# Cross-attention phase of a four-layer decoder kernel: order of SyncE's loads and stores, place of the residual on GpSimd, and order of two VectorE steps

## Chip, cores and metric

One Trainium2 chip, one core. The metric is the device time of one execution in microseconds (us). The kernel before was timed in three runs: median 3507.88 us, from 3506.46 to 3513.25 us. Step numbers (h), rounds (r) and line numbers below are those of the kernel before.

## The reference

Four decoder layers are applied one after the other to `x` (32 sequences of 128 tokens, 256 features), each with a context of the same shape. Layer 0 is the one in which the change lies. It has 8 heads of 128 features, and this form (cut down):

```python
Q, K, V = linear(x), linear(x), linear(x)                 # inner projections
x  = layer_norm(x0 + mha(Q, K, V, causal and pad mask))   # self attention
Q2 = linear(x); K2 = linear(context); V2 = linear(context)
y  = layer_norm(x0 + mha(Q2, K2, V2, pad mask))           # cross attention
ff = linear(relu(linear(y)))                              # 256 -> 1024 -> 256
x  = layer_norm(y + ff)
```

where `mha` projects to 8 heads, computes `softmax(q k^T / sqrt(128))` with masked keys at minus infinity, mixes the values and projects back to 256 features. `x0` is the input of the layer in both residual sums. Layers 1 to 3 (16 heads of 16 features) follow and are not touched.

## The kernel before, in words

**Phases.** `four_layers` runs four phases in turn, each a block with a program for every engine, with a barrier between them: `phase8` with `cross=False` (layer 0, self attention), `phase8` with `cross=True` (layer 0, cross attention and feed-forward; tiles named `cross_...`), then the phases `middle` and `fourth`. The diff touches `phase8`, and only what it does under `cross`.

**Rounds.** The cross phase has 8 rounds (0 to 7) of 4 sequences, that is 512 tokens. Rounds 0, 1 and 7 (`LAST`) are written out, 2 to 6 are a hardware loop on each engine. In round r the engines do three things at once, interleaved by hand in `one_round`: attention of round r, the first layer norm and the feed-forward of round r-1, and the second layer norm of rounds r-1 and r-2. Matmuls are split for precision: every operand is a high and a low part, and `product` (L90 to L99) makes three matmuls for one, all recorded as L97.

**One step h of TensorE (PE)** (h = 0 to 7, one per head, L1288 to L1329): scores of head h (L365, after a mask matmul L359); V and then K projection for head i = h+2 (`pe_v`, `pe_head`, reading the context tiles `ct_hi`, `ct_lo`); a feed-forward slot; the Q projection for head i (reading `xt_hi`, `xt_lo`); turn of the probabilities of head h (`pe_turn`, L374, four transposes); a slot; output projection of head h-1 (`pe_out`); at some h the transposes of a layer norm (L562); a slot; mix with V (`pe_mix`, L385). At h = 6 and 7 the index i wraps, and the projections are those of the next round: at h = 6 PE waits for `ct_loaded` ahead of V and for `x_loaded` ahead of Q. Feed-forward slots exist from h = 2 on, three to a step (`slot_of`): slot s makes output piece `out_of(s)` and then hidden piece `hidden_of(s)`. There are 16 hidden pieces t.

**PSUM banks** in this phase: V in bank 4, K and Q share bank 3, but Q of steps h = 0 and 1 goes to bank 2 (`spare`). Hidden pieces take banks 4, 4, 3 in turn (`HID`), so slot 12 (h = 6) writes bank 4, out of which VectorE must have taken V before. Bank 2 also holds the feed-forward output; output piece t = 8 (slot 11, h = 5) may only begin when VectorE has read the sum of pair 0 out of it (`sum2`, L179, tile `cross_z`). A claim of a bank is a wait for its last reader.

**VectorE (DVE) in a step** (L1023 to L1060): `dve_max` (L450, the row maxima of the scores), eviction of V (`dve_v`, L437), eviction of K (`dve_k`, L444), then `dve_weigh`, which takes the reciprocal of the softmax sums (L457) and multiplies the probabilities (L460, two inputs in SBUF). It waits for the exponentials on ScalarE (L417, four with an accumulator read each). PE's turn waits for L460. At h = 6 the evictions of V and K come behind `dve_weigh`. Then follow casts of hidden pieces to their high part (`dve_hi`, L531), norm sums and statistics, and last `dve_lo` (L466).

**GpSimd (POOL) in a round** (`one_round`, L1187 to L1215): three small operations for `poison`, the normalisation of the norms (`pool_hat`, L202, L205, L210), then for each hidden piece t its low part (`pool_lo`, L536), and between them `rows1`, `rows2` (L219 and L227) and, behind t = 9, `make_residual`: two TENSOR_TENSOR operations over 128x1024 (L1157 adds the output bias to `x_rows`, L1162 adds `poison`). The first of them releases `residual_sum`, the second `residual_ready`, for which VectorE waits in `sum1` at h = 0 of the next round. Behind t = 14 comes `make_flags` for the next round (L1129), behind t = 15 `rows2(Back(r, 1), 0)`.

**SyncE (SP)** issues every DMA in program order, and a wait on it holds all that is behind it. In round r of the loop: `load_round(r+1)`, then `store_rows(r-2, pair 1)`, `store_columns(r-2)`, `store_rows(r-1, pair 0)`. `load_round` under `cross` waits and issues in this order: pad (waits for `pad_flags`), `x_rows` (L765, waits for `residual_sum` of round r), context high and low (L772, wait until V and K of round r are all projected, that is for K of h = 5), x high and low (L777, wait for Q of h = 5). The two context loads are 512 KB each, as are the two of x and the two of `store_columns`. `store_columns(r-2)` waits for `norm2.lo_ready`, whose last part VectorE makes at h = 4 of round r (L587), and `store_rows(r-2, pair 1)` for `rows2` behind t = 8.

Of the kernel before, what the change touches and what calls it, by code (L numbers as in the profile page):

```python
# [85 lines left out]
def f32(ap):  # L86
    return ap.bitcast(F32)
# [564 lines left out]
def phase8(nc, tag, cross, x, ctx_t, pad, packed, cols, v_row_dram, rows, out, ctx_out, to_flag=()):  # L652
# [3 lines left out]
    with ExitStack() as ctx:  # L656
# [94 lines left out]
        def _(sp):  # L751
            def load_round(r):
                tok = bass.ds(r * TOK, TOK)
                if not cross:
# [4 lines left out]
                sp.wait_ge(pad_flags.sem, pad_flags.at(r, 0))  # L759
                kit.gated(sp)  # L760
                sp.dma_start(pad_ints[:], pad[bass.ds(r * G, G)].rearrange("b o k -> o b k")
                             .broadcast_to([P, G, SEQ])).then_inc(pad_loaded.sem, 16)
                sp.wait_ge(residual_sum.sem, residual_sum.at(r, 0))
                kit.gated(sp)
                sp.dma_start(x_rows[:], x[-1][tok, :].rearrange("(b t) f -> t b f", b=G)) \  # L765
                  .then_inc(rows_loaded.sem, 16)
                if cross:
                    sp.wait_ge(att.v_in_psum.sem, att.v_in_psum.at(r, 0))
                    sp.wait_ge(att.k_in_psum.sem, att.k_in_psum.at(r, 0))
                    kit.gated(sp)  # L770
                    for tile, src in ((ct.hi, ctx_t[0]), (ct.lo, ctx_t[1])):
                        sp.dma_start(f32(tile[:]), src[:, tok].rearrange("(c p) t -> p c t", p=P)) \  # L772
                          .then_inc(ct_loaded.sem, 16)
                    sp.wait_ge(att.q_in_psum.sem, att.q_in_psum.at(r, 0))
                    kit.gated(sp)
                    for tile, src in ((xt.hi, x[0]), (xt.lo, x[1])):
                        sp.dma_start(f32(tile[:]), src[:, tok].rearrange("(c p) t -> p c t", p=P)) \  # L777
                          .then_inc(x_loaded.sem, 16)
# [73 lines left out]
            else:  # L852
                load_round(1)
                load_round(2)
                store_rows(0, 1, 1, 0)
                with sp.Fori(2, LAST) as r:
                    load_round(r + 1)
                    store_rows(Back(r, 2), r, 2, 1)
                    store_columns(Back(r, 2), r, 2)
                    store_rows(Back(r, 1), r, 1, 0)  # L860
# [99 lines left out]
        def _(dve):  # L960
# [48 lines left out]
            def one_round(r, post, tail, more):  # L1009
# [3 lines left out]
                for h in range(H8):  # L1013
# [9 lines left out]
                    if cross and project and h != H8 - 2:  # L1023
                        att.dve_k(dve, r, psum, i, ahead)
# [2202 lines left out]
```

## Time and profile before

| what | value |
|---|---|
| three timed runs | 3506.46, 3507.88, 3513.25 us |
| the profiled execution's own time | 3517.44 us, 9.6 us above the median |
| its span | 3515.7 us |
| time outside the span | 1.7 us |
| granted clock of PE, mean of the span | 0.956 of full speed |
| busy, share of the span | PE 88%, DVE 56%, ACT 56%, POOL 47% |
| cross phase, from its first load (620.6 us) to its last store (1477.8 us) | 857 us |

How to read it: all times in the rows are us from the start of the span unless marked ns. "PE" is the matmul side of TensorE and "PEld" its weight loads, which overlap it. A time in square brackets is the idle time of that engine just before the instruction, and behind the arrow stands what ended it. Matmuls are pipelined: a row's own duration is longer than the step to the next matmul's start, so an idle time counted from the end of one to the start of the next is somewhat less than what the chain of starts loses. The granted clock is the share of full speed (2.4 GHz) at which PE ran; 0.5 is its lower level, 1.2 GHz.

### The profile page before, as it was taken

Reading aid. Unit: us, or ns where it says so; the run is one execution under the profiler, and the core shown is the slowest. Engines: PE = TensorE matmul, PEld = TensorE weight load, DVE = VectorE, ACT = ScalarE, POOL = GpSimd, SP = SyncE. Lnnn points to the kernel's source line nnn. Section 1 sums busy time; section 2 is a strip of 40 time slices with the busy share of each in tenths; the row PEclk is TensorE's granted clock in tenths of the full one; section 3 lists DMA queues with packets and bytes.
Section 4 is the critical chain, followed back from the end, with each engine's and each line's share of the span. In section 5 each row is a group of like instructions: output and inputs, shape, how many; then the busy total and the mean of one; then the engine's idle time right before and its main releaser. Section 6 shows DMA issues by size and latency. Waiting matters only on the chain. (4 is left out here: it accounts for less than half of the span.)

```text
span 3515.7 us, 81973 instructions
## 1 busy us (share of the span) xinstructions
PE 3087.0 (88%) x28275; PEld 2679.8 (76%) x28400; DVE 1985.9 (56%) x4082; ACT 1961.5 (56%) x7922; POOL 1648.8 (47%) x2002
## 2 busy tenths in 40 slices
PE   7999997799999999537999999999999999848886
PEld 5999997488888889536888888788888888745564
DVE  2455554344444444335777777777777777635665
ACT  2444443233344444226777777777777777626775
POOL 1233333114444444512566666666666666652445
PEclk8999998899999999868999999999999999979998
DMA  2222221401111110032221222233111111122321
GB/s 100 64 69 66 78 72 37 147 28 37 52 51 45 51 50 19 36 110 73 82 70 59 67 68 70 86 90 112 58 56 58 59 54 56 36 74 65 102 85 56
DMA packets 218094, 232.77 MB, mean 66 GB/s; under 512 B 41920, under 2 KB 183232, under 8 KB 215360
## 3 DMA queue, kind: packets, MB, share of 16 engines
q1 hardware_dynamic: 217920, 230.49, 20.8%
q8 instruction: 105, 1.72, 0.2%
q14 instruction: 69, 0.57, 0.1%
HBM read 148.57 MB, written 65.01 MB: 61 GB/s over the span
## 5 line engine op out<-in xcount | busy, mean ns | idle before, releaser
L1719 ACT ACTIVATE middle_stage<-middle_psum,middle_neg_max 128x128 f32<-128x128 f32 x2048 | 727.7, 386 | 358.5 <-DVE middle_neg_max L1699 358.2
L1719 ACT ACTIVATION_READ_ACCUMULATOR middle_stage<-middle_psum,middle_neg_max 128x1 f32 x2048 | 462.2, 226 | 0.0
L1699 DVE TENSOR_REDUCE middle_neg_max<-middle_psum 128x4 f32<-128x512 f32 x512 | 337.4, 681 | 63.0 <-PE middle_psum L1662 62.9
L1673 PE MATMUL middle_psum<-middle_eye,middle_stage 128*128 128x128 f32 x2048 | 322.1, 280 | 19.2 <-DVE middle_p_turned_odd L1705 9.4
L1673 PEld LDWEIGHTS middle_psum<-middle_eye,middle_stage 128*128 128x128 f32 x2048 | 232.5, 142 | 71.0 <-issue 46.5
L1621 POOL COPY middle_inverse_row<-middle_inverse 128x128 f32<-128x128 f32 x256 | 68.6, 297 | 381.6 <-DVE middle_inverse L1588 348.5
L1786 POOL TENSOR_SCALAR middle_n_z<-middle_n_z,middle_n_moments,middle_n_rstd 128x256 f32<-128x256 f32 x192 | 234.7, 1229 | 20.3 <-POOL middle_n_rstd L1781 20.3
L536 POOL TENSOR_TENSOR cross_ff_hidden_lo<-cross_ff_relu,cross_ff_hidden_hi 128x256 fp32r<-128x256 f32 x128 | 101.2, 792 | 284.9 <-DVE cross_ff_hidden_hi L531 284.9
L1901 POOL TENSOR_TENSOR middle_ff_hidden_lo<-middle_ff_relu,middle_ff_hidden_hi 128x256 fp32r<-128x256 f32 x256 | 184.2, 740 | 52.8 <-DVE middle_ff_hidden_hi L1895 52.8
L97 PE MATMUL middle_psum<-middle_n_yt_hi,middle_w_lo 128*128 128x256 f32 x640 | 194.7, 304 | 14.4 <-DVE middle_n_yt_lo L1833 9.7
L1705 DVE COPY middle_p_turned_odd<-middle_psum 128x512 f32<-128x512 f32 x256 | 174.8, 683 | 34.4 <-PE middle_psum L1673 34.3
L1705 DVE COPY middle_stage<-middle_psum 128x512 f32<-128x512 f32 x256 | 175.5, 685 | 20.8 <-PE middle_psum L1673 20.5
L1600 ACT ACTIVATE fourth_stage<-fourth_psum,fourth_neg_max 128x128 f32<-128x128 f32 x512 | 182.1, 387 | 4.1 <-DVE fourth_neg_max L1576 4.1
L97 PE MATMUL middle_psum<-middle_n_yt_hi,middle_w_hi 128*128 128x256 f32 x640 | 179.8, 281 | 0.0
L97 PE MATMUL middle_psum<-middle_n_yt_lo,middle_w_hi 128*128 128x256 f32 x640 | 179.6, 281 | 0.0
L1628 POOL TENSOR_TENSOR middle_attended_lo<-middle_mix,middle_attended_hi 128x256 fp32r<-128x256 f32 x128 | 95.0, 742 | 160.2 <-DVE middle_attended_hi L1711 160.2
L97 PE MATMUL middle_psum<-middle_w_hi,middle_ff_hidden_lo 128*128 128x256 f32 x512 | 163.7, 320 | 3.5 <-POOL middle_ff_hidden_lo L1901 3.5
L531 DVE CAST cross_ff_hidden_hi<-cross_ff_relu 128x256 fp32r<-128x256 f32 x128 | 44.6, 349 | 215.8 <-ACT cross_ff_relu L526 215.8
L526 ACT ACTIVATE cross_ff_relu<-cross_psum,cross_cols 128x256 f32<-128x256 f32 x128 | 60.8, 475 | 178.5 <-PE cross_psum L97 178.5
L1662 PE MATMUL middle_psum<-middle_stage,middle_a_q 32*128 32x256 f32 x2048 | 152.3, 413 | 0.3 <-ACT middle_stage L1719 0.2
L97 PE MATMUL middle_psum<-middle_w_lo,middle_ff_hidden_hi 128*128 128x256 f32 x512 | 145.0, 283 | 0.0
L97 PE MATMUL middle_psum<-middle_w_hi,middle_ff_hidden_hi 128*128 128x256 f32 x512 | 144.7, 283 | 0.0
(341 smaller groups left out, 10880.7 us busy)
## 6 DMA issues: line engine op xcount, KB each, us to landing
middle_stage<-middle_a_k SPq DMA_DIRECT2D x1024, 16.0 KB, 1.8
middle_xt_hi<-x_hi SPq DMA_DIRECT2D x32, 256.0 KB, 2.7
middle_xt_lo<-x_lo SPq DMA_DIRECT2D x32, 256.0 KB, 3.0
middle_ct_hi<-context_hi SPq DMA_DIRECT2D x32, 256.0 KB, 2.9
middle_ct_lo<-context_lo SPq DMA_DIRECT2D x32, 256.0 KB, 3.2
middle_x_rows<-x_rows SPq DMA_DIRECT2D x32, 256.0 KB, 2.8
middle_mask_flags<-flags SPq DMA_DIRECT2D x128, 64.0 KB, 1.9
x_rows<-middle_n_z SPq DMA_DIRECT2D x32, 256.0 KB, 2.2
```

Of the source, the lines that this page charges most:

```text
L97: ins = pe.matmul(out, w, x, start=first and n == 0, stop=last and n == total - 1, skip_group_check=skip)
L536: pool.tensor_tensor(self.hidden.lo[:, t % HIDDEN_SLOTS, :], self.relu[:, t % HIDDEN_SLOTS, :], f32(self.hidden.hi[:, t % HIDDEN_SLOTS, :] ...
L1600: ins = act.activation(self.sh.p[:, h % 4, x, :], psum[:, SCORE_BANKS[h % 4], x * SEQ:(x + 1) * SEQ], ACT.Exp, bias=self.sh.neg_max[:, h % ...
L1621: ins = pool.tensor_copy(self.sh.inverse_row[:, b, k * P:(k + 1) * P].rearrange("p (g d) -> p g d", g=8), self.sh.inverse[:, b, k * 8:(k + ...
L1628: pool.tensor_tensor(self.sh.attended.lo[:, :, b * SEQ:(b + 1) * SEQ], self.sh.mix[:, b, :].rearrange("p (c q) -> p c q", c=C), f32(self.s ...
L1662: ins = pe.matmul(banks.psum[:, bank, c * T2:(c + 1) * T2].rearrange("p (e k) -> p e k", e=2), self.proj.q[rows, c, tokens], self.proj.k_b ...
L1673: ins = pe.transpose(banks.psum[:, TURN_BANK, x * SEQ:(x + 1) * SEQ], self.sh.p_wide[:, 4 * b + t, x, :], self.sh.eye[:])
L1699: dve.tensor_reduce(self.sh.neg_max[:, 4 * b + t, :], psum[:, SCORE_BANKS[t], :].rearrange("p (x k) -> p x k", x=4), AX_X, ALU.max, negate ...
L1705: dve.tensor_copy(self.sh.p_turned_of[b][:, t, :, :], psum[:, TURN_BANK, :].rearrange("p (x k) -> p x k", x=4)) \
L1719: ins = act.activation(self.sh.p_wide[:, 4 * b + t, x, :], psum[:, SCORE_BANKS[t], x * SEQ:(x + 1) * SEQ], ACT.Exp, bias=self.sh.neg_max[: ...
L1786: pool.tensor_scalar(self.z[:, b, :], self.z[:, b, :], self.moments[:, b, 0:1], self.rstd[:, b:b + 1], ALU.subtract, ALU.mult) \
L1901: pool.tensor_tensor(self.hidden.lo[:, slot, :], self.relu[:, slot, :], f32(self.hidden.hi[:, slot, :]), ALU.subtract).then_inc(self.lo_re ...
```

## The change

Four edits, all under `cross`:

1. SyncE: `load_round` is cut into `load_inputs` (context, then x), `load_pad` and `load_rows`. In the rounds 1 and 2 and in the loop they come in the order inputs, pad, rows, with the stores between them. In the loop `store_columns(r-2)` is the first thing, `load_inputs(r+1)` the second, and `load_rows(r+1)` the last.
2. GpSimd: `make_residual(r)` moves from behind t = 9 to behind t = 15, ahead of `rows2(Back(r, 1), 0)`. In round 0, which has no feed-forward, it stays.
3. VectorE: at h = 0 and 1 `dve_weigh` comes ahead of the eviction of K instead of behind it.
4. The start of the phase (`load_round(0)`) and the stores of the last rounds are the same as before.

```diff
--- before.py
+++ after.py
@@ -749,6 +749,33 @@
 
         @block.sync
         def _(sp):
+            def load_inputs(r):
+                tok = bass.ds(r * TOK, TOK)
+                sp.wait_ge(att.v_in_psum.sem, att.v_in_psum.at(r, 0))
+                sp.wait_ge(att.k_in_psum.sem, att.k_in_psum.at(r, 0))
+                kit.gated(sp)
+                for tile, src in ((ct.hi, ctx_t[0]), (ct.lo, ctx_t[1])):
+                    sp.dma_start(f32(tile[:]), src[:, tok].rearrange("(c p) t -> p c t", p=P)) \
+                      .then_inc(ct_loaded.sem, 16)
+                sp.wait_ge(att.q_in_psum.sem, att.q_in_psum.at(r, 0))
+                kit.gated(sp)
+                for tile, src in ((xt.hi, x[0]), (xt.lo, x[1])):
+                    sp.dma_start(f32(tile[:]), src[:, tok].rearrange("(c p) t -> p c t", p=P)) \
+                      .then_inc(x_loaded.sem, 16)
+
+            def load_pad(r):
+                sp.wait_ge(pad_flags.sem, pad_flags.at(r, 0))
+                kit.gated(sp)
+                sp.dma_start(pad_ints[:], pad[bass.ds(r * G, G)].rearrange("b o k -> o b k")
+                             .broadcast_to([P, G, SEQ])).then_inc(pad_loaded.sem, 16)
+
+            def load_rows(r):
+                tok = bass.ds(r * TOK, TOK)
+                sp.wait_ge(residual_sum.sem, residual_sum.at(r, 0))
+                kit.gated(sp)
+                sp.dma_start(x_rows[:], x[-1][tok, :].rearrange("(b t) f -> t b f", b=G)) \
+                  .then_inc(rows_loaded.sem, 16)
+
             def load_round(r):
                 tok = bass.ds(r * TOK, TOK)
                 if not cross:
@@ -756,26 +783,10 @@
                     kit.gated(sp)
                     sp.dma_start(x_raw[:], x[0][:, tok].rearrange("(c p) t -> p c t", p=P)) \
                       .then_inc(x_raw_loaded.sem, 16)
-                sp.wait_ge(pad_flags.sem, pad_flags.at(r, 0))
-                kit.gated(sp)
-                sp.dma_start(pad_ints[:], pad[bass.ds(r * G, G)].rearrange("b o k -> o b k")
-                             .broadcast_to([P, G, SEQ])).then_inc(pad_loaded.sem, 16)
-                sp.wait_ge(residual_sum.sem, residual_sum.at(r, 0))
-                kit.gated(sp)
-                sp.dma_start(x_rows[:], x[-1][tok, :].rearrange("(b t) f -> t b f", b=G)) \
-                  .then_inc(rows_loaded.sem, 16)
+                load_pad(r)
+                load_rows(r)
                 if cross:
-                    sp.wait_ge(att.v_in_psum.sem, att.v_in_psum.at(r, 0))
-                    sp.wait_ge(att.k_in_psum.sem, att.k_in_psum.at(r, 0))
-                    kit.gated(sp)
-                    for tile, src in ((ct.hi, ctx_t[0]), (ct.lo, ctx_t[1])):
-                        sp.dma_start(f32(tile[:]), src[:, tok].rearrange("(c p) t -> p c t", p=P)) \
-                          .then_inc(ct_loaded.sem, 16)
-                    sp.wait_ge(att.q_in_psum.sem, att.q_in_psum.at(r, 0))
-                    kit.gated(sp)
-                    for tile, src in ((xt.hi, x[0]), (xt.lo, x[1])):
-                        sp.dma_start(f32(tile[:]), src[:, tok].rearrange("(c p) t -> p c t", p=P)) \
-                          .then_inc(x_loaded.sem, 16)
+                    load_inputs(r)
                 else:
                     sp.wait_ge(ct_lo.sem, ct_lo.at(r, 0))
                     kit.gated(sp)
@@ -850,14 +861,20 @@
                 for m in makers:
                     sp.wait_ge(m.stored.sem, m.stored.at(ROUNDS, 0))
             else:
-                load_round(1)
-                load_round(2)
+                load_inputs(1)
+                load_pad(1)
+                load_rows(1)
+                load_inputs(2)
+                load_pad(2)
                 store_rows(0, 1, 1, 0)
+                load_rows(2)
                 with sp.Fori(2, LAST) as r:
-                    load_round(r + 1)
+                    store_columns(Back(r, 2), r, 2)
+                    load_inputs(r + 1)
                     store_rows(Back(r, 2), r, 2, 1)
-                    store_columns(Back(r, 2), r, 2)
+                    load_pad(r + 1)
                     store_rows(Back(r, 1), r, 1, 0)
+                    load_rows(r + 1)
                 store_rows(LAST - 2, LAST, 2, 1)
                 store_columns(LAST - 2, LAST, 2)
                 store_rows(LAST - 1, LAST, 1, 0)
@@ -1020,12 +1037,12 @@
                         att.dve_v(dve, r, psum, i, ahead)
                     if cross and post and h == 2:
                         norm1.dve_lo_in(dve, Back(r, 1), 0, 0)
-                    if cross and project and h != H8 - 2:
+                    if cross and project and h not in (0, 1, H8 - 2):
                         att.dve_k(dve, r, psum, i, ahead)
                     att.dve_weigh(dve, r, h)
                     if project and h == H8 - 2:
                         att.dve_v(dve, r, psum, i, ahead)
-                    if project and (not cross or h == H8 - 2):
+                    if project and (not cross or h in (0, 1, H8 - 2)):
                         att.dve_k(dve, r, psum, i, ahead)
                     if cross and post:
                         hidden_hi(Back(r, 1), slot_of(h, 0))
@@ -1208,10 +1225,9 @@
                             norm1.rows(pool, Back(r, 1), pair)
                     elif t == 8 and tail:
                         rows2(Back(r, 2), 1)
-                    elif t == 9:
-                        make_residual(r)
                     elif t == 14 and more:
                         make_flags(r, 1)
+                make_residual(r)
                 rows2(Back(r, 1), 0)
 
             if not cross:
```

## Rows read from the trace of the kernel before

**Rows 1.** PE's waits, cross phase: waiter, releaser: us in total, times, longest us.

```profile
PE cross_psum L97 <- DMA cross_ct_lo<-context_lo: 18.0, 6, 4.0
...
PE cross_psum L374 <- DVE cross_arena L460: 10.2, 18, 2.0
...
PE cross_psum L97 <- DVE cross_z L179: 6.2, 7, 0.9
```

**Rows 2.** Six windows from turn (h=0) to turn, rounds 1 to 7: sum and mean.

```profile
sum 577.88, PE 546.95 PEld 512.03 DVE 256.26 ACT 238.77 POOL 251.30; mean PE 91.16 PEld 85.34 DVE 42.71 ACT 39.79 POOL 41.88
```

**Rows 3.** Timeline of SP, round 3: start us, us, queue, line, transfer.

```profile
1016.45 0.40 SPq L765 DMA_DIRECT2D cross_x_rows<-in_x_rows  x1
```

**Rows 4.** Timeline of PE, round 3, steps 5 and 6.

```profile
1006.90 1.05 PE L365 MATMUL cross_psum<-cross_k,cross_q 128*128 128x128 f32 x8
...
1007.71 0.36 PE L97 MATMUL cross_psum<-cross_w_hi,cross_ct_lo 128*128 128x256 f32 x1
...
1011.33 0.28 PE L97 MATMUL cross_psum<-cross_yt_hi,cross_w_lo 128*128 128x256 f32 x1
...
1019.66 1.05 PE L365 MATMUL cross_psum<-cross_k,cross_q 128*128 128x128 f32 x8
...
1023.22 0.58 PE L97 MATMUL cross_psum<-cross_w_hi,cross_ct_lo 128*128 128x256 f32 x1 [2.51 <-DMA cross_ct_lo<-context_lo]
```

**Rows 5.** Windows: us, busy PE, PEld, DVE, ACT, POOL, PE clock, DMA, GB/s.

```profile
746.00:750.00 4.00, 4.00 (x20) 3.73 (x19) 0.00 (x0) 1.27 (x2) 0.00 (x0) 0.57 0.00 0
...
1023.00:1026.50 3.50, 3.28 (x14) 3.21 (x15) 1.19 (x3) 0.09 (x1) 1.02 (x1) 0.53 1.04 366
...
1120.30:1125.50 5.20, 5.15 (x19) 4.63 (x20) 0.69 (x1) 0.00 (x0) 0.00 (x0) 0.52 0.84 312
```

**Rows 6.** Timeline of round 0, step 5 (load) and step 6.

```profile
734.17 0.38 SPq L772 DMA_DIRECT2D cross_ct_hi<-context_hi  x1
...
740.18 0.36 PE L97 MATMUL cross_psum<-cross_w_hi,cross_ct_lo 128*128 128x256 f32 x1
...
743.66 0.68 DVE L437 TENSOR_TENSOR cross_arena<-cross_psum,cross_v_row 128x512 f32<-128x512 f32 x1
...
745.15 0.47 PE L97 MATMUL cross_psum<-cross_xt_hi,cross_w_lo 128*128 128x512 f32 x1 [1.91 <-DVE cross_k L444]
```

**Rows 7.** DMA issues, window 1112 to 1117 (round 4): KB, us to landing.

```profile
cross_ct_lo<-context_lo SPq DMA_DIRECT2D x1, 512.0 KB, 6.9
```

**Rows 8.** Line L531 (ns min/median/max), then the timeline of round 3, step 5.

```profile
L531 DVE CAST cross_ff_hidden_hi<-cross_ff_relu x95: 293/294/1062, 783.3 to 1326.4; 128x256 fp32r<-128x256 f32 x95
...
1013.82 2.39 POOL L1157 TENSOR_TENSOR cross_residual<-cross_x_rows,cross_rows 128x1024 f32<-128x1024 f32 x1
...
1016.37 1.89 POOL L1162 TENSOR_TENSOR cross_residual<-cross_residual,cross_poison 128x1024 f32<-128x1024 f32 x1 [0.16 <-POOL cross_residual L1157]
...
1015.30 1.06 DVE L531 CAST cross_ff_hidden_hi<-cross_ff_relu 128x256 fp32r<-128x256 f32 x1 [2.25 <-ACT cross_ff_relu L526]
...
1017.01 0.39 PE L97 MATMUL cross_psum<-cross_w_hi,cross_ff_hidden_lo 128*128 128x256 f32 x1 [0.88 <-DVE cross_z L179]
```

**Rows 9.** Timeline of round 3, step 0: exponentials, Q matmuls, weighing, turn.

```profile
955.98 0.22 ACT L417 ACTIVATION_READ_ACCUMULATOR cross_arena<-cross_psum,cross_neg_max 128x1 f32 x1
...
957.10 0.39 PE L97 MATMUL cross_psum<-cross_xt_lo,cross_w_hi 128*128 128x512 f32 x1
...
957.26 0.69 DVE L460 TENSOR_TENSOR cross_arena<-cross_arena,cross_inverse 128x512 f32<-128x512 f32 x1
...
957.33 0.39 PE L97 MATMUL cross_psum<-cross_xt_hi,cross_w_hi 128*128 128x512 f32 x1
...
958.10 0.63 PE L374 MATMUL cross_psum<-cross_eye,cross_arena 128*128 128x128 f32 x4 [0.38 <-DVE cross_arena L460]
```

**Rows 10.** Timeline of POOL: first norm of round 3, first norm behind round 7.

```profile
961.58 0.22 POOL L202 TENSOR_SCALAR cross_n_variance<-cross_n_moments 128x2 f32<-128x2 f32 x1 [6.26 <-DVE cross_n_moments L193]
...
1428.19 0.23 POOL L202 TENSOR_SCALAR cross_n_variance<-cross_n_moments 128x2 f32<-128x2 f32 x1 [3.75 <-DVE cross_n_moments L193]
```

## The prediction

> **What bounds the kernel now.** I first read the waits of PE alone over the cross phase [rows 1], since nothing outside this phase is edited. The reader is to see that three releasers hold nearly all of PE's idle time there: a DMA into `cross_ct_lo` (18.0 us in 6 waits), the weighed probabilities of L460 (10.2 us in 18 waits) and the sum L179 (6.2 us in 7 waits). Then come the six windows from one turn at h = 0 to the next [rows 2]: a round takes 577.88 / 6 = 96.3 us, PE is busy for 91.2 us of it, VectorE for 42.7, GpSimd for 41.9. So PE is the bound, what takes idle time off PE shortens the round one for one, and the other engines have over 50 us of room in each.
>
> The three waits have their places. **Context.** In round 3 SP issues `x_rows` at 1016.45 [rows 3], and the context stands behind it in the program. `x_rows` waits for the residual, whose first operation on POOL ends at 1013.82 + 2.39 = 1016.2 [rows 8]. The V projection of step 6, which needs the context, starts 3.56 us behind the scores (1019.66 to 1023.22), where in step 5 it is 0.81 us (1006.90 to 1007.71) [rows 4]. So 2.75 us of PE's chain of starts are lost where the row says 2.51 us idle: 0.24 us more than the idle time. Behind it, the granted clock is 0.53 for 3.5 us in round 3 and 0.52 for 5.2 us in round 4 [rows 5]: PE, after having waited, works at its lower level of 1.2 GHz. **Sum.** The cast L531 takes 294 ns in the median of 95 and 1062 ns at most; the long one (1015.30) runs beside L1157 on POOL (1013.82 to 1016.21) and ends just behind it; L179 comes behind the cast on VectorE, and PE waits 0.88 us for it [rows 8]. **Turn.** At h = 0 the exponentials are done at 956.20, but the eviction of K, which waits for PE, stands ahead of the weighing, and the turn starts 0.77 us behind the last Q matmul (957.33 to 958.10) [rows 9], where these matmuls otherwise start 0.23 us apart (957.10, 957.33).
>
> **The change part by part, and its sum.**
>
> *Weighing first at h = 0 and 1.* With the exponentials done at 956.20, L457 and L460, which take 0.9 us from the end of K's eviction to their own end at 957.95 [rows 9], end at about 957.2, before the turn could start unheld, 957.33 + 0.23 = 957.56. So each wait gives 0.77 - 0.23 = 0.54 us. Of the 18 waits of [rows 1] two, of 2.0 us each, are in round 7 at h = 6 and 7 and not touched; 16 are of this kind (two in each of 8 rounds): 16 x 0.54 = **8.6 us**. The evicted K comes about 0.8 us later; nothing waits: Q of these steps goes to bank 2, bank 3 is claimed a step later, and the scores of head h + 2 are two steps off. Bounds: 0 (the chain over ScalarE's turned copy binds instead) and 8.6; I take 8.6, as the copy is followed by a mix with 12 output matmuls between.
>
> *Residual at the round's end.* In step 5 the cast takes 0.29 instead of 1.06 us, L179 starts 0.77 us earlier, and PE's wait of 0.88 shrinks by that: 7 x 0.77 = **5.4 us**. Its new place is free of casts: none follows hidden piece 15 before h = 2 of the next round. Its length there is 4.4 us (1013.82 to 1016.37 + 1.89 [rows 8]). POOL was idle 6.26 us before the next norm at 961.58 [rows 10], so `rows2`, the poison and the residual end at about 959.7 at the latest, the residual ahead of `rows2` and the poison, some 3 us earlier. `sum1`, with its statistics and moments, lies about 2 us ahead of 961.58, so the residual is on time. Behind round 7 the idle time is 3.75 us only [rows 10], and the norms of the drain, on which PE waits, begin 4.40 - 3.75 = **0.65 us later**, once. Bounds of this: 0 and 4.4.
>
> *Context and x first.* V and K of step 5 are done before the hidden piece at 1011.33 [rows 4]. From there SP needs about 0.5 us to the second issue; landing takes 6.9 us at most (round 4, with `x_rows` and the stores beside it) [rows 7]. That is 1018.7 at the latest; V is wanted at 1007.71 + (1019.66 - 1006.90) = 1020.47, less the 0.77 of above, 1019.7. Round 0 is the specimen: `x_rows` was long loaded there, the context was issued at 734.17, and V at 740.18 did not wait [rows 6]. `store_columns` now stands ahead, but what it waits for is made at h = 4, about 10 us earlier. x waits for Q of step 5 and is wanted by Q of step 6; both lie a hidden piece and more behind K and V, so it has the context's margin again. Pad now comes behind these and is wanted 20 us later; `x_rows` is issued a round's length before its use. So the six waits go, with their surplus: 18.0 + 6 x 0.24 = 19.4 us.
>
> *What is late next.* At h = 6 VectorE weighs first and then evicts V and K. Until now the DMA hid this. In round 0, V starts at 740.18 and is evicted at 743.66 + 0.68 = 744.34, 4.16 us later; PE sees an eviction about 0.15 us after its end. The hidden piece of slot 12 takes V's bank, and unheld it would start 1011.33 - 1007.71 = 3.62 us behind V. So PE waits 4.16 + 0.15 - 3.62 = 0.69 us. Q needs K out, at 745.15 - 740.18 = 4.97 us behind V [rows 6]; with the hidden piece (about 0.7 us) between, this holds no further. Price 6 x 0.69 = 4.1 us. Bounds: 0, as in all steps up to 5, and 1.91 us each, as in round 0, where no feed-forward piece fills the gap. Net of this part 19.4 - 4.1 = **15.3 us**.
>
> *The clock.* The loss is the window times (1 - clock): 3.5 x 0.47 = 1.65 us in round 3 (1, 2, 5 and 6 are like it) and 5.2 x 0.48 = 2.5 us in round 4 [rows 5]: 5 x 1.65 + 2.5 = **10.8 us**, if the lower clock goes with the wait. It was also at 0.57 in round 0 behind the wait of 1.91 us (746 to 750), which stays; after waits of 0.88 us the trace has no drop. The new wait of 0.69 us lies on this side, so I count the whole.
> The Trainium skill, in "TensorE: Matmul & The Clock Gate", section "A second HAM failure mode: psum-queue depth-cycling", tells of a kernel in which brief idling of PE between groups of matmuls, often enough, made the clock swing. By that rule the drops would stay with the shorter wait, and the sum would be about 29 instead of 39.5 us; this trace speaks against it where only short waits occur, the sixteen turns.
>
> **Sum:** 8.6 + 5.4 - 0.65 + 15.3 + 10.8 = 39.5 us. The profiled execution took 3517.4 us and should come to 3477.9. It stands 9.6 us above the median of the three runs; from the median, 3507.9 - 39.5 = **3468.4 us**, 1.1% faster. A measurement of this kernel can tell about 0.2% (7 us) from no change. A round should go from 96.3 to about 90.1 us.
>
> **Rivals.**
> 1. *The clock still drops.* The wait of 0.69 us at h = 6, or 1.91 us if the evictions run as in round 0, takes the clock down as before. For it: 1.91 us did so in round 0. Against: 0.88 us never did. Time: 39.5 - 10.8 = 28.7 us gained, 3479.2 us. The skill's rule above is this case. Chance 0.10.
> 2. *The loads are not ahead of need* (the change does not do what it says): `store_columns` at the head of the queue holds them, or they land as late by contention. Then only the weighing and the residual count: 8.6 + 5.4 - 0.65 = 13.4 us, 3494.5 us. Against: the store's condition is met at h = 4. Chance 0.05.
> 3. *The chain of a step binds, not PE.* Scores, maximum, exponentials, weighing and turn take the place of each removed wait and the time stays at 3508 us. Against: from h = 2 to 5 PE has no wait longer than the 0.88 us. Chance 0.03.
> 4. *Slower: the residual is late.* `sum1` at h = 0 waits for a residual made at the round's end, VectorE's maximum of head 1 waits behind `sum1`, and PE's turn behind that. Every us by which the residual misses `sum1` costs each of seven rounds 1 us; slower than before from 39.5 / 7 = 5.6 us late on. By the rows it is over 3 us early. 8 us late would give 56 - 39.5 = 16 us slower, 3525 us. Chance 0.02.
>
> **How the numbers follow.** The forecast has 0.80. Its own range is 3460 (no new wait at h = 6, +4.1 us, and some us of scatter, which the three runs show) to 3478 (the new wait at the round-0 size, 6 x 1.2 = 7.3 us, and the drain's 4.4). The low end stays at 3460; the upper end goes to 3483 to take in the first rival with its scatter. The second, third and fourth are left out. Faster by over 0.2%: 0.95 (forecast and rivals 1 and 2); within: 0.03; slower: 0.02.
>
> **What would show it.** In PE's waits of the changed kernel: no DMA wait on the context; L374 down to its two waits of 2.0 us; L97 behind L179 at about 0.1 us each; new, six waits of about 0.7 us on the eviction of V (L437) at h = 6. In the windows: granted clock 1.00 from round 1 to 6. L531 with a maximum near 0.3 us. On SP: the context issued about 9 us ahead of V. It would be wrong if the clock stayed at 0.5 once a round, if the new wait at h = 6 were near 2 us, or if DVE waited for `cross_residual` at h = 0.

## The result, and the profile after

| | kernel before | changed kernel |
|---|---|---|
| median of the timed executions | 3508.28 us (3506.46 to 3513.25, 4) | 3477.12 us (3469.61 to 3478.37, 4) |
| ratio of the medians, 95% interval | | 0.9901 (0.9886 to 0.9916) |
| the profiled execution | 3517.44 us | 3477.88 us |

The changed kernel is faster by 31.2 us between the medians and by 39.6 us between the two profiled executions. The forecast was 3468.4 us (3460 to 3483), 39.5 us less, and the profiled execution at 3477.9. The 8 us between the two ways of counting are taken up below (`a_changed`, `b_before`). The first rival's 3479.2 us lies nearer to the median than the forecast does, so the time alone can't tell the two apart; the granted clock does.

The page of the changed kernel, head and first part:

```profile
span 3476.2 us, 81973 instructions
...
PE 3076.5 (89%) x28275; PEld 2675.0 (77%) x28400; DVE 1980.9 (57%) x4082; ACT 1959.7 (56%) x7922; POOL 1653.2 (48%) x2002
```

PE's waits in the cross phase of the changed kernel (waiter, releaser: us in total, times, longest us), to be held against [rows 1]. This window ends ahead of the drain, in round 7:

```profile
PE cross_psum L97 <- DVE cross_k L444: 6.1, 6, 1.9
PE cross_psum L374 <- DVE cross_arena L460: 4.4, 3, 2.0
PE cross_psum L97 <- DVE cross_arena L437: 2.6, 6, 0.4
PE cross_psum L385 <- ACT cross_p_turned L424: 0.8, 1, 0.8
PE cross_psum L97 <- DVE cross_yt_lo L587: 0.3, 1, 0.3
```

The DMA wait (18.0 us) and the wait on L179 (6.2 us) are gone. L374 is down from 18 waits to 3: the two of 2.0 us in round 7, and one of 0.3 us in round 0. In their place stands the wait that was said to be late next, six times 0.43 us on the eviction of V (L437). The six behind K's eviction (L444) are all in round 0 and were there before.

Three views answer to [rows 3, 4, 7]. First, the timeline of SP in round 3 of the changed kernel:

```profile
985.52 0.39 SPq L831 DMA_DIRECT2D x_hi<-cross_y_out_hi  x1
...
994.94 0.39 SPq L758 DMA_DIRECT2D cross_ct_hi<-context_hi  x1
995.43 0.42 SPq L758 DMA_DIRECT2D cross_ct_lo<-context_lo  x1
997.70 0.37 SPq L763 DMA_DIRECT2D cross_xt_hi<-x_hi  x1
...
1031.60 0.37 SPq L776 DMA_DIRECT2D cross_x_rows<-in_x_rows  x1
```

The timeline of PE in the same round, step 6:

```profile
1002.82 1.05 PE L365 MATMUL cross_psum<-cross_k,cross_q 128*128 128x128 f32 x8
1003.63 0.36 PE L97 MATMUL cross_psum<-cross_w_hi,cross_ct_lo 128*128 128x256 f32 x1
...
1007.85 0.39 PE L97 MATMUL cross_psum<-cross_yt_hi,cross_w_lo 128*128 128x256 f32 x1 [0.43 <-DVE cross_arena L437]
```

The DMA view of the window 1085 to 1089 (round 4; KB, us from issue to landing):

```profile
cross_ct_lo<-context_lo SPq DMA_DIRECT2D x1, 512.0 KB, 4.7
```

The context is issued 8.7 us ahead of V (994.94 to 1003.63), and V starts 0.81 us behind the scores, as in step 5. In this window the context lands in 4.7 us where it took 6.9 us. Over rounds 1 to 6 it is 4.5 to 5.3 us where it was 5.4 to 6.9 us; `x_rows` and the three stores that followed at once are no longer beside it, and which of them counts was not tried. The hidden piece of slot 12 starts 4.22 us behind V instead of 3.62.

The timeline of VectorE around the cast of step 5, against [rows 8]:

```profile
999.24 0.29 DVE L531 CAST cross_ff_hidden_hi<-cross_ff_relu 128x256 fp32r<-128x256 f32 x1 [2.25 <-ACT cross_ff_relu L526]
999.45 0.68 DVE L179 TENSOR_TENSOR cross_z<-cross_psum,cross_y_rows 128x512 f32<-128x512 f32 x1
```

The timeline of GpSimd at the end of round 3, up to the next norm, against [rows 10]:

```profile
1023.62 2.40 POOL L1174 TENSOR_TENSOR cross_residual<-cross_x_rows,cross_rows 128x1024 f32<-128x1024 f32 x1
1026.18 1.90 POOL L1179 TENSOR_TENSOR cross_residual<-cross_residual,cross_poison 128x1024 f32<-128x1024 f32 x1 [0.16 <-POOL cross_residual L1174]
...
1036.47 0.22 POOL L202 TENSOR_SCALAR cross_n_variance<-cross_n_moments 128x2 f32<-128x2 f32 x1 [4.75 <-DVE cross_n_moments L193]
```

The cast has its 0.29 us back. The residual is done at 1028.1, `sum1` begins at 1034.46, as soon as PE is ready, and GpSimd still idles 4.75 us ahead of the norm. L531 does not quite keep to 0.3 us: the longest of rounds 1 to 6 takes 498 ns, five of them about that long beside L210 on GpSimd, and no wait of PE follows.

One round from context issue to context issue, in the changed kernel (us, busy PE, PEld, DVE, ACT, POOL, granted clock, DMA, GB/s):

```profile
904.69:994.94 90.25, 89.20 (x659) 84.06 (x666) 42.15 (x90) 39.83 (x116) 43.93 (x46) 1.00 0.14 50
```

A round takes 90.3 us where it took 96.3 [rows 2], and the clock is full.

### The profile page after: what moved, and what is told of

The parts are those of the page before. It is cut to its first block and busy times, and to the rows that moved or that the text cites. A ratio compares the mean times of both kernels' runs of the same rounds, so it can differ in the third digit from the quotient of the medians.

```text
span 3476.2 us, 81973 instructions
## 1 busy us (share of the span) xinstructions
PE 3076.5 (89%) x28275; PEld 2675.0 (77%) x28400; DVE 1980.9 (57%) x4082; ACT 1959.7 (56%) x7922; POOL 1653.2 (48%) x2002
## 5 line engine op out<-in xcount | busy, mean ns | idle before, releaser
L97 PE MATMUL middle_psum<-middle_n_yt_hi,middle_w_lo 128*128 128x256 f32 x640 | 195.1, 305 | 14.7 <-DVE middle_n_yt_lo L1849 10.0
L97 PE MATMUL middle_psum<-middle_n_yt_hi,middle_w_hi 128*128 128x256 f32 x640 | 180.6, 282 | 0.0
L97 PE MATMUL middle_psum<-middle_n_yt_lo,middle_w_hi 128*128 128x256 f32 x640 | 180.2, 282 | 0.0
L97 PE MATMUL middle_psum<-middle_w_hi,middle_ff_hidden_lo 128*128 128x256 f32 x512 | 164.2, 321 | 3.5 <-POOL middle_ff_hidden_lo L1917 3.5
L531 DVE CAST cross_ff_hidden_hi<-cross_ff_relu 128x256 fp32r<-128x256 f32 x128 | 40.8, 319 | 214.9 <-ACT cross_ff_relu L526 214.8
L97 PE MATMUL middle_psum<-middle_w_lo,middle_ff_hidden_hi 128*128 128x256 f32 x512 | 145.3, 284 | 0.0
L97 PE MATMUL middle_psum<-middle_w_hi,middle_ff_hidden_hi 128*128 128x256 f32 x512 | 145.1, 283 | 0.0
```

The lines of the kernel that those rows point to most:

```text
L97: ins = pe.matmul(out, w, x, start=first and n == 0, stop=last and n == total - 1, skip_group_check=skip)
```

## How the experiments are read

The change has three edits: SyncE's order ("SP" below), the residual's place and the weighing's place. The self, middle and fourth phases are not edited, but they scatter: over the traces of this study the self phase ended between 610 and 621 us, and the start of the cross phase took 63 to 71 us. So beside the medians stands the **stretch of rounds**: from the first to the last weight load of the mask matmul (L359, once a head, 64 in all), that is from round 0 to step 7 of round 7. This is the line in the kernel before (min/median/max ns, first and last start):

```profile
L359 PEld LDWEIGHTS cross_psum<-cross_flags,cross_masked_eye x64: 95/100/100, 685.8 to 1415.7; 128*128 128x128 bf16 x64
```

And in the changed kernel:

```profile
L359 PEld LDWEIGHTS cross_psum<-cross_flags,cross_masked_eye x64: 95/100/100, 683.4 to 1374.8; 128*128 128x128 bf16 x64
```

729.9 and 691.4 us: the edited code gained 38.5 us. What lies outside the stretch took from 2777 to 2788 us in the 13 traces. "Half clock" below is the time in this stretch at the lower level (1.2 GHz). It is there for 3.4 us at a time, or for 6.8 us, called two pieces. A piece costs about 1.6 us: the changed kernel has one at h = 6 of round 0 and `a_changed` has not, and that step is 1.60 us longer. The text below counts a piece as 1.7 us, half of its length, which is an upper bound, as PE may stand idle for part of it.

The starts of L359 also give every single step, from one head to the next. Between the first two traces the sixteen steps h = 0 and 1 gained 8.6 us, the seven steps h = 5 gained 5.4 us and the six steps h = 6 of rounds 1 to 6 gained 24.9 us. All others together lost 0.4 us.

| kernel | edits | stretch, us | half clock, us | median, us | before, same set of runs |
|---|---|---|---|---|---|
| before / `b_before` | none | 729.9 / 730.3 | 27.3 / 30.7 | - / (3516.3, one) | - / 3513.2 |
| `e1_weigh_only` | weighing | 715.1 | 13.7 | 3501.4 | 3512.2 |
| `e2_loads_only` | SP | 705.7 | 3.4 | 3490.2 | 3512.2 |
| `e3_loads_residual` | SP, residual | 699.8 | 3.4 | 3483.7 | 3512.2 |
| `e4_loads_weigh` | SP, weighing | 695.5 | 0 | 3479.3 | 3512.2 |
| changed / `a_changed` | all | 691.4 / 691.2 | 3.4 / 3.4 | 3477.1 / 3470.5 | 3508.3 / 3509.6 |
| `g1_wait_1` | all, longer wait | 695.4 | 3.4 | (3479.4, one) | 3509.6 |
| `g2_wait_2` | all, still longer | 699.1 | 6.8 | (3488.4, one) | 3513.2 |
| `f1_v_first` | all, V ahead of the weighing at h = 6 | 686.1 | 0 | 3471.6 | 3509.6 |
| `f2_round0` / `f3_round0_again` | as `f1_v_first`, and round 0 | 681.3 / 681.1 | 3.4 / 3.4 | 3461.5 / 3464.6 | 3509.6 / 3513.2 |

The median of `f2_round0` is that of three executions; a fourth took 16496 us, and with it the median is 3465.0 us.

The residual alone, without the SP edit, was not tried: by the order of the program the context loads would wait for a residual that is made behind work which itself needs them, and the kernel would stand still.

## One part at a time

**`e1_weigh_only`**, the kernel before with this:

```diff
-                    if cross and project and h != H8 - 2:
+                    if cross and project and h not in (0, 1, H8 - 2):
                         att.dve_k(dve, r, psum, i, ahead)
                     att.dve_weigh(dve, r, h)
...
-                    if project and (not cross or h == H8 - 2):
+                    if project and (not cross or h in (0, 1, H8 - 2)):
                         att.dve_k(dve, r, psum, i, ahead)
```

> The kernel before with VectorE's edit alone (weighing ahead of K at h = 0 and 1). My theory: the turn waits L374 fall from 18 to about 2, 8.6 us less than before; the six context waits and the lower clock behind them stay. Rival (the chain of a step binds): the waits come back elsewhere and the time stays that of before. A second rival: the waits on the context grow by what the turns give, because the loads are released by GpSimd and do not come earlier with PE; then only the part of round 0 and 7 is left, 1 to 2 us.

Measured: 3501.36 us, ratio 0.9962 (0.9947 to 0.9977), 10.8 us less than before; the stretch 14.8 us less. Of these, 1.6 us are smaller DMA waits (16.4 for 18.0 us, the row below) and up to 6.8 us are four pieces of half clock fewer, so at least 6.4 us are the weighing. Step by step it is 8.6 us, the sum of the sixteen steps h = 0 and 1. The turn waits of 0.4 us are gone but for one of 0.3 us. The context waits stayed, as the theory had it; neither rival held.

```profile
PE cross_psum L97 <- DMA cross_ct_lo<-context_lo: 16.4, 6, 3.6
```

This is its row in the view of PE's waits. That these waits came with less half clock was not expected. Windows of 20 us around the six waits (the columns are those of the windows above):

```profile
815.00:835.00 20.00, 16.61 (x115) 15.42 (x115) 7.14 (x15) 5.63 (x16) 9.01 (x10) 0.91 0.38 132
910.00:930.00 20.00, 15.44 (x105) 14.35 (x105) 6.90 (x15) 4.69 (x15) 8.77 (x10) 0.91 0.56 198
1005.00:1025.00 20.00, 16.59 (x113) 15.34 (x114) 7.16 (x15) 5.50 (x17) 9.58 (x10) 0.91 0.56 197
1100.00:1120.00 20.00, 16.18 (x124) 15.24 (x124) 7.16 (x15) 6.58 (x19) 9.28 (x10) 1.00 0.55 197
1195.00:1215.00 20.00, 16.87 (x116) 15.93 (x118) 6.04 (x14) 6.61 (x18) 8.07 (x9) 0.91 0.57 197
1290.00:1310.00 20.00, 17.17 (x131) 16.45 (x134) 7.02 (x17) 7.27 (x19) 8.81 (x11) 1.00 0.55 197
```

In the fourth and the sixth the clock stayed full; the waits there are 2.88 and 2.48 us. The first of them in PE's timeline:

```profile
1108.53 0.38 PE L97 MATMUL cross_psum<-cross_w_hi,cross_ct_lo 128*128 128x256 f32 x1 [2.88 <-DMA cross_ct_lo<-context_lo]
```

**`e2_loads_only`**, the changed kernel with `make_residual` back behind t = 9 and K evicted first at all h, so that SyncE's edit alone is left:

> The kernel before with SyncE's edit alone: residual behind t = 9, K evicted first. My theory: the six waits of 18 us and the lower clock (six windows) vanish, six waits of 0.43 us on the eviction of V come: 15.3 + 10.8 = 26 us less than before. Rival (the lower clock has nothing to do with the wait): 15 us less, and the clock still at 0.5 once a round.

Measured: 3490.20 us, ratio 0.9934 (0.9920 to 0.9948), 22.0 us less; the stretch 24.2 us less. No DMA wait is left, six of 0.43 us on L437 are there, and the clock is low once, for 3.4 us in round 0. Loads and clock were put at 26 us; measured 24 to 22. The rival (15 us, the clock still low once a round) is out: with the waits the half clock went from 27.3 to 3.4 us.

**`e3_loads_residual`**, the changed kernel with the diff of `e1_weigh_only` reversed:

> The changed kernel with VectorE's edit undone. My theory: 8.6 us more than the changed kernel, sixteen turn waits of 0.39 us are back. Rival (the median gained 31 and not 39.5 us because the weighing is worth nothing outside the profiled run): the same time as the changed kernel within 2 us.

Measured: 3483.67 us; its stretch is 8.4 us longer than that of the changed kernel, with the same half clock. 8.6 us was the term. Between `e2_loads_only` and `e4_loads_weigh` the weighing gives 10.2 us, of which 1.7 us are the one piece of half clock: 8.5 us. The rival, a time within 2 us of the changed kernel, is out.

**`e4_loads_weigh`**, the changed kernel with

```diff
+                    elif t == 9:
+                        make_residual(r)
                     elif t == 14 and more:
                         make_flags(r, 1)
-                make_residual(r)
```

> The changed kernel with the residual put back behind t = 9. My theory: the cast L531 is at 1.06 us once a round again and L179 holds PE for 0.88 us in seven rounds: 5.4 us more, less 0.65 us that the drain gets back, so 4.8 us more than the changed kernel; the SP queue is unaffected. Rival (the cast is long for another reason than L1157 beside it): no change, or the long cast stays in the changed kernel too.

Measured: 3479.32 us; its stretch is 4.1 us longer than the changed kernel's although it has one piece of half clock less, so up to 5.8 us for the residual's place in the rounds (5.4 forecast). The seven steps h = 5 alone, where the cast lies, are 5.3 us longer than in `a_changed`. L531 in this kernel, rounds 1 to 6 (min/median/max ns):

```profile
L531 DVE CAST cross_ff_hidden_hi<-cross_ff_relu x99: 293/294/1062, 775.0 to 1327.6; 128x256 fp32r<-128x256 f32 x99
```

And in the changed kernel:

```profile
L531 DVE CAST cross_ff_hidden_hi<-cross_ff_relu x99: 293/294/498, 779.1 to 1327.1; 128x256 fp32r<-128x256 f32 x99
```

The long cast comes and goes with the residual beside it, and so do the seven waits on L179 (6.2 us in this kernel, none in the changed one).

## Does the gain stand, and why do the first medians show less of it

**`a_changed`**, the changed kernel unedited:

> The changed kernel once more, unedited, to stand beside the next two on the same chip. My theory: the stretch from the first score step of round 0 to the last of round 7 takes 691.4 us as in its first profile (729.9 before), whatever the phases that were not edited do; in total 37 to 40 us less than the kernel before. Rival (the gain is the 31 us of the first medians, and the profiled pair flattered it): the same stretch takes 697 us or more, or the total is 31 us less.

Measured: 3470.49 us (3470.16 to 3472.89) beside 3509.55 us for the kernel before, ratio 0.9889 (0.9873 to 0.9906): 39.1 us. The stretch is 691.2 us. Here the total is what the theory says. The edited stretch is the same to 0.2 us in both traces of the changed kernel (each has one piece of half clock, the first in round 0, the second in round 7), while the spans, 3476.2 and 3468.7 us, differ by 7.5 us. So code that was not edited scatters by as much as the first median fell short. That it did so in the first set of runs is likely, but not shown, since only the profiled executions have traces.

**`b_before`**, the kernel before unedited:

> The kernel before once more, unedited, for a second trace. My theory: the stretch of rounds takes 729.9 us within some us; how many windows at the lower clock lie in rounds 1 to 6 (seven with the double one in the first trace) moves it by 1.7 us each; the phases that were not edited differ by up to 10 us, which is why the first profiled execution stood 9.6 us above its median. Rival: the stretch itself is near 722 us, and the sum of 39.5 us rested on an odd trace.

Measured: one execution of 3516.3 us; the stretch 730.3 us. Its half clock is 30.7 us: the seven pieces of rounds 1 to 6 and the one of round 0 as in the first trace, and one more in round 7, behind a turn wait of 2.03 us. The context waits sum to 16.0 us where the first trace has 18.0. So the sum did not rest on an odd trace. Which unedited phase made the first profiled execution 9.6 us longer than the median can't be said, since the timed executions of before have no traces.

## The wait that is late next, and the clock

**`g1_wait_1`**, the changed kernel with V evicted behind K at h = 6:

```diff
+                    if project and h == H8 - 2 and not (cross and post):
                         att.dve_v(dve, r, psum, i, ahead)
                     if project and (not cross or h in (0, 1, H8 - 2)):
                         att.dve_k(dve, r, psum, i, ahead)
+                    if project and h == H8 - 2 and cross and post:
+                        att.dve_v(dve, r, psum, i, ahead)
```

> The changed kernel with K evicted ahead of V at h = 6, so that the wait of hidden piece 12 grows by one eviction, from 0.43 to about 1.1 us in six rounds: 4 us more. On the clock, theory (short waits of PE up to about 1 us do not lower it): granted clock 1.0 in rounds 1 to 6 as in the changed kernel. Rival (any wait at h = 6 longer than before lowers it, as the Trainium skill's section on a second failure mode of the clock gate would have it): 0.5 for some us once a round, and some 14 us more.

Measured, in one execution: six waits of 1.1 us, 6.5 us in all, the stretch 4.0 us longer, and no low clock in rounds 0 to 6. So the wait has the cause that was given, and 1.1 us does not lower the clock here. The rival is out for this length.

**`g2_wait_2`**, the same with a reduction over the flags into a scratch tile between K and V (its output is used by nothing):

```diff
+                    if project and h == H8 - 2 and cross and post:
+                        dve.tensor_reduce(scratch[:], sh.flags[:], AX_X, ALU.min) \
+                           .then_inc(scratch_made.sem, 1)
+                        dve.wait_ge(scratch_made.sem, scratch_made.at(r, 0))
```

> The kernel of g1_wait_1 with one more reduction on VectorE (over the flags, into a scratch tile) ahead of the eviction of V at h = 6, in six rounds, so that the wait of PE there grows to about 1.8 us, as long as the one of round 0 behind which the clock fell in two of the traces so far and did not in three. Theory (a wait of this length lowers the clock in some rounds and not in others): 0.5 for 3.4 us in one to five of the six rounds, 1.7 us each on top of the 8 us that the waits themselves cost over the changed kernel. Rival 1 (only waits on a DMA lower it): 1.0 throughout. Rival 2 (always): six windows, 18 us over the changed kernel.

Measured, in one execution, first the row of PE's waits:

```profile
PE cross_psum L97 <- DVE cross_arena L437: 10.9, 6, 1.8
```

Then windows around three of the six waits:

```profile
1010.00:1026.00 16.00, 14.13 (x95) 13.05 (x95) 4.99 (x10) 5.83 (x17) 4.95 (x7) 0.89 0.01 6
1190.00:1210.00 20.00, 18.02 (x126) 16.74 (x127) 6.92 (x17) 6.84 (x19) 6.27 (x8) 0.91 0.24 82
1280.00:1300.00 20.00, 18.02 (x134) 16.79 (x134) 7.41 (x18) 7.56 (x20) 7.01 (x9) 1.00 0.37 130
```

The clock fell behind two of the six waits of 1.8 us, and these are waits on VectorE, not on a DMA; both rivals are out. The stretch is 7.7 us longer than the changed kernel's, less than the 8.3 us by which the waits grew. Round by round against `a_changed`, the four rounds without a low clock are 1.0 us longer and the two with it 2.6 and 2.7 us, so a fall of the clock costs 1.6 us. The growth of a wait by 1.4 us costs only 1.0 us, as other steps of the same round are some hundredths to 0.13 us shorter; why was not followed up.

**`f1_v_first`**, the changed kernel with V evicted ahead of the weighing at h = 6:

```diff
-                    if project and h != H8 - 2:
+                    if project and (cross and post or h != H8 - 2):
                         att.dve_v(dve, r, psum, i, ahead)
...
-                    if project and h == H8 - 2:
+                    if project and h == H8 - 2 and not (cross and post):
                         att.dve_v(dve, r, psum, i, ahead)
```

> The changed kernel with V evicted ahead of the weighing at h = 6, in the rounds with a feed-forward. My theory (the wait that is late next is the V eviction behind the weighing): the six waits of 0.43 us of L97 behind L437 vanish, 6 x 0.67 = 4.0 us less in the stretch of rounds. Rival (hidden piece 12 is held by something else right behind, such as K's eviction for Q): another wait of about the same size takes its place and the time is that of the changed kernel.

Measured: the six waits on L437 are gone and nothing of their size came; the context issues of this kernel follow each other at 89.70 us where `a_changed` has 90.32. The stretch is 5.1 us shorter, 1.7 of it a piece of half clock that `a_changed` had in round 7: 3.4 us for a forecast of 4.0. The median, 3471.59 us, can't tell it from `a_changed` (3470.49 us): 4 us is less than the other phases scatter. The two profiled spans are 3469.5 and 3468.7 us, so all that lies outside the stretch took 5.9 us more in this one.

**`f2_round0`**, `f1_v_first` with bank 2 for every Q of round 0, and the weighing ahead of K in all of round 0:

```diff
-                        att.act_q(act, r, psum, (h + 2) % H8, (h + 2) // H8)
+                        att.act_q(act, r, psum, (h + 2) % H8, (h + 2) // H8,
+                                  FF8_OUT_BANK if cross and not post else None)
...
-                        att.pe_head(pe, r, banks, "q", q_src, i, ahead)
+                        att.pe_head(pe, r, banks, "q", q_src, i, ahead,
+                                    FF8_OUT_BANK if cross and not post else None)
...
-                    if cross and project and h not in (0, 1, H8 - 2):
+                    if cross and project and post and h not in (0, 1, H8 - 2):
                         att.dve_k(dve, r, psum, i, ahead)
...
-                    if project and (not cross or h in (0, 1, H8 - 2)):
+                    if project and (not cross or not post or h in (0, 1, H8 - 2)):
                         att.dve_k(dve, r, psum, i, ahead)
```

> The kernel of f1_v_first with, in round 0, every Q projection in bank 2 and every weighing ahead of K's eviction. My theory: the five waits of 0.84 us and the one of 1.90 us behind K's eviction (L444) go, each worth its idle time and 0.16 us, together 7 us, and with the lower clock behind the last of them (3.4 us at half speed, 1.7 us) up to 9 us less than f1_v_first. Rival (the softmax chain of round 0 binds, as no feed-forward fills the steps): the turn waits for the weighing instead and at most 3 us come.

Measured: 3461.5 us over three executions, ratio 0.9872 (0.9852 to 0.9891). The stretch is 4.8 us shorter than that of `f1_v_first` with one piece of half clock more, so 6.5 us for a forecast of 7, and the rival (3 us at most) is out. The other 1.7 us had nothing to come from, as `f1_v_first` had no low clock in round 0. The fourth execution, of 16496 us, has no trace, and its cause is open.

**`f3_round0_again`**, the same kernel:

> The kernel of f2_round0 unedited, since one of its four timed executions lay far outside the others. Theory (a disturbance of that one execution): all executions between 3455 and 3475 us. Rival (the kernel itself can stall): another one far out.

Measured: 3464.62 us (3461.93 to 3469.03, 4 executions), ratio 0.9865 (0.9848 to 0.9881). The long execution did not come again in four. That speaks for a disturbance but does not prove one. The waits that are left up to round 7 (L375, L386, L462, L468 and L589 are L374, L385, L460, L466 and L587 of the kernel before):

```profile
PE cross_psum L375 <- DVE cross_arena L462: 4.4, 3, 2.0
PE cross_psum L386 <- ACT cross_p_turned L426: 0.8, 1, 0.8
PE cross_psum L97 <- DVE cross_attended_lo L468: 0.7, 1, 0.7
PE cross_psum L97 <- DVE cross_yt_lo L589: 0.6, 2, 0.3
PE cross_psum L97 <- DMA cross_xt_lo<-x_lo: 0.4, 1, 0.4
```

These are 6.9 us, where the same view of the kernel before has 42 us. This version is the fastest of the study, 48.6 us below the kernel before on its chip.

## Why the prediction was right, point by point

- **PE is the bound**, and what leaves its waits leaves the time. Right: 30 us of waits and their clock gone, 2.6 us of new waits, and 38.5 us off the stretch. The third rival is out.
- **Weighing first, 8.6 us.** Right: 8.4 and 8.5 us in the two pairs that differ by it alone, 8.6 us in its own steps. One of the sixteen waits stayed, 0.3 us in round 0, where the exponentials themselves are late.
- **Residual at the round's end, 5.4 us.** Right, 5.3 us in its own steps and 5.8 us at most over the stretch. L97 behind L179, forecast at 0.1 us each, shows no wait. The rival of a late residual is out: it lies 6 us ahead of `sum1`.
- **The drain, 0.65 us later.** The mechanism is seen. GpSimd now runs from `rows2` into the first norm without idling, and PE waits 4.57 us for it; the kernel before waited 4.01 us. The timeline of GpSimd behind round 7:

```profile
1387.83 0.23 POOL L202 TENSOR_SCALAR cross_n_variance<-cross_n_moments 128x2 f32<-128x2 f32 x1
```

The timeline of PE there:

```profile
1391.66 1.02 PE L562 MATMUL cross_psum<-cross_eye,cross_z 128*128 128x128 f32 x4 [4.57 <-POOL cross_z L210]
```

  That is 0.56 us. Of the eight traces with the residual at the round's end six have 4.54 to 4.64 us here; `e3_loads_residual` and `f1_v_first` have 4.04 and 4.00, and in both the clock fell after the last turn of round 7, behind which PE comes later. The five traces with the residual behind t = 9 have 4.01 to 4.03 us. No total shows it, since the drain scatters by 3 us.
- **Loads first, 19.4 us less the new wait of 4.1 us, and the clock's 10.8 us.** Right within 2 to 4 us: 24.2 us of stretch and 22.0 of median for 26.1. The six steps h = 6, where all of it lies, gained 24.9 us in the changed kernel. My estimate of the split: single pieces of half clock at 1.56 us (round 0 of the kernel before against `e1_weigh_only`) and the double one of round 4 at 2.2 us (3.31 us of step less 1.12 us of wait, same pair) give 10.0 us for the clock, forecast at 10.8, and leave 14.9 us for the waits, forecast at 15.3. The second rival is out, as `store_columns` was issued 9.4 us ahead of the context. The new wait came at its place with its price: 0.60 us of the chain of starts for 0.69. The row shows 0.43 us idle; the forecast of "about 0.7 us" in the view of waits was the start-to-start figure and belonged 0.24 us lower, by the same correction that I had made for the DMA wait.
- **The first rival (the clock still drops)** did not happen in rounds 1 to 6 of any kernel with waits up to 1.1 us. The Trainium skill, in "TensorE: Matmul & The Clock Gate", section "A second HAM failure mode: psum-queue depth-cycling", tells of a kernel whose clock swung under frequent short idling of PE. Here the six waits of 0.43 us of the changed kernel and the six of 1.1 us of `g1_wait_1` left the granted clock at 1.00 in rounds 1 to 6.
- **The median.** 3477.1 for 3468.4 us. The weak step is taking the whole difference of profiled executions over to the first median. It held in the later set of runs (39.1 us); in the first, 8 us were missing, as much as the code outside the edited stretch scatters. The range of 23 us covered it, and so did the forecast's own range, by 1 us. That range had a slip: its terms at the upper end, 7.3 us for the new wait and 4.4 for the drain in place of 0.65, give 3479.5 and not 3478 us.

## What to carry to other kernels

Where one queue issues all transfers, a wait in it is a wait of everything behind; put first what is needed soonest, and behind it what has a round of time, and price each wait by the chain of starts plus the clock it drags down. Ask of each removed wait what it was hiding: here an eviction order that had cost nothing became the next wait, within a tenth of a us of what the old trace gave. Measure a gain of 1% over the stretch that was edited; totals carry the scatter of phases that were not.

## What was not expected of the hardware

The clock does not fall behind every wait of PE of a given length. Behind the waits on the context (2.15 to 4.0 us) it fell in 12 of 12 in the two traces of the kernel before, but in 4 of 6 in `e1_weigh_only`, where 2.46 us lowered it and 2.88 us did not, and where one wait of 2.48 us did and another did not. Behind the wait of 1.9 us in round 0 it fell in 5 of the 11 traces that have it, and behind the six of 1.8 us in `g2_wait_2` in 2. Behind the two turn waits of 2.03 to 2.05 us at the end of round 7, which all 13 traces have, it fell in 8 of 26. Behind waits up to 1.1 us it never did. What decides it between two waits of one length stays open. So a price for the clock taken from one trace is the price of a chance: 10.8 us was near for two traces of the kernel before, at most 6.8 us would have been for `e1_weigh_only`.
